# A four-layer graph network on one core: the vectors' pair products of the last two node parts move from VectorE to GpSimd, and their three-component sum is made by TensorE transposes

## The chip, the cores and the metric

The kernel is one program on one core of a Trainium2 chip. The metric is the device time of one execution in microseconds (us), lower is better. A core has five engines that run their own instruction streams and meet only at semaphores: TensorE (PE, matmuls and transposes into PSUM), VectorE (DVE), ScalarE (ACT), GpSimd (POOL) and SyncE (SP, which here only issues DMAs).

## What is computed

Four graph layers follow each other over 6,250 nodes and 206,250 edges. A node has 160 features: 64 scalars and 32 vectors of 3 components. Each layer ends in a residual and a layer norm. The last two layers (called L2 and L3 in the reference) have an edge part, which sums messages into each node, and a node part, which multiplies every node's own features with what it received. The node part of L3, cut to what matters:

```
a0 = agg[:, :64]                       # received scalars
a1 = agg[:, 64:].reshape(n, 32, 3)     # received vectors
xs = node_features[:, :64]
xv = node_features[:, 64:].reshape(n, 32, 3)
u0 = einsum('nu,nv,uvw->nw', xs, a0, Wu_ss) * INV64
   + einsum('nui,nvi,uvw->nw', xv, a1, Wu_vv) * (INV_SQRT3 * INV32)
u1 = einsum('nu,nvi,uvw->nwi', xs, a1, Wu_sv) * INV_SQRT2048
   + einsum('nui,nv,uvw->nwi', xv, a0, Wu_vs) * INV_SQRT2048
u0 = u0 + xs @ Lu_s * INV8
u1 = u1 + einsum('nui,uw->nwi', xv, Lu_v) * INV_SQRT32
x  = layernorm(x + node_features + update)
```

The term of this study is the second one of `u0`: for every node, the products of 32 own vectors with 32 received vectors, component by component, summed over the 3 components and then contracted with `Wu_vv`. L2 has the same term.

## The kernel before

The two node parts are two calls of `nodes_update`, named n3 and n4 (the trace writes both as `n_`). Each call goes over 50 blocks of 128 nodes, two blocks per turn of a hardware loop (`run_steps`). The engines' programs are software pipelined over blocks: in a step with number s, TensorE, VectorE, ScalarE and GpSimd do the front of block s, the products of block b = s - 1 and the end of block p = s - 2. Nothing but semaphores and the order in which each engine's program is written sets the order.

For one block b, with its 128 nodes on the 128 partitions:

- **Scalar pairs.** VectorE forms `n_ss`, the 64 x 64 products of own and received scalars, in four pieces of 1024 (`pair_products`, L1940). TensorE turns each piece by 128 x 128 transposes into `n_ps_s` (`turn_half`, L1803), ScalarE copies that to `n_turnedT` (L1899), and TensorE contracts it with the weights `n_WQ` into `n_ps_l` (`contract_half`, L1814). Two halves h come from each piece, so h runs from 0 to 7.
- **Vector pairs.** VectorE forms `n_vv`, 3 x 32 x 32 products, in one instruction of 3072 elements per partition (L1945). TensorE makes two more halves of it, h = 8 and 9: each 128 x 128 column block of each of the three components is multiplied with the identity, and the three products add up in PSUM (L1807). Copy and contraction follow as for the other halves.
- **End of block p** (`finish`, on VectorE). The sums of block p are added up into `n_y` (L1954, L1958), then comes the layer norm: statistics (L739, L741, L742), the inverse root on GpSimd (`inverse_root`, L757, a power of -0.5), and `n_new` (L747), which reads `n_y` and the statistics and waits for GpSimd's root.
- **Vector outputs** (`vector_products`, on VectorE). Two times: two products of a PSUM tile `n_ps_z` with a broadcast operand (L1974) and a reduction of 3072 elements to 48 (L1979). TensorE fills `n_ps_z` in `columns` (L1827).
- **Front of block s.** SP loads its rows into `n_row` (L1753), after L1954 of block p, which used that buffer. GpSimd copies the block's received sums into `n_own` (L1918), TensorE transposes both (`front`, L1774 to L1778), and `messages` (L1787, L1789) makes `n_agg`.

VectorE's program in a step is therefore `pair_products(b)`, `finish(p)`, `vector_products(b)`. GpSimd's is the copy of `n_own` for s and the root for p:

```
if s.exists():
    if s.reuses(2):
        pool.wait_ge(turned, s.count(-1))
    pool.tensor_copy(own[s.j][:, :], acc[:, bass.ds(s.t() * CAT, CAT)]).then_inc(held, 1)
p = s.back(2)
if p.exists():
    inverse_root(pool, stats[p.j][:, 8:9], power[:, 0:1], squares, roots, p, 1, 1)
```

In TensorE's program `turn_half(b, h + 1)` stands ahead of `contract_half(b, h)`; the front of s comes after h = 6, and `columns(b, 2)`, `columns(b, 3)` and `messages(s)` after h = 7.

Of the kernel before, what the change touches and what calls it, by code (L numbers as in the profile page):

```python
# [8 lines left out]
ALU = mybir.AluOpType  # L9
# [3 lines left out]
P = 128  # L13
# [8 lines left out]
CS, CV = 64, 32  # L22
D = CS + 3 * CV
# [66 lines left out]
def run_steps(eng, step, lag, unroll, number, held=(), peel=1):  # L90


    turns = number // unroll
    assert turns * unroll == number and lag <= unroll
    for i in range(peel):
        for j in range(unroll):
            step(Tile(i, j, unroll, number))
    with eng.Fori(peel, turns) as i:
        registers = {(a, c): eng.snap(eng.to_reg(i * a + c)) for a, c in held} or None
        for j in range(unroll):  # L100
            step(Tile(i, j, unroll, number, 0, registers))
    for j in range(lag):
        step(Tile(turns, j, unroll, number))
# [10 lines left out]
def bcast(ap, shape):  # L114
    return ap.to_broadcast(list(shape))
# [634 lines left out]
def layernorm(dve, chain, y, stats, out, squares, roots, item, nth, each):  # L750
    moments(dve, chain, y, stats, squares)
    return normalise(dve, y, stats, out, roots, item, nth, each)


def inverse_root(pool, at, power, squares, roots, item, nth, each):
    pool.wait_ge(squares, item.count(nth, each))
    pool.tensor_tensor(at, at, power, ALU.pow).then_inc(roots, 1)  # L757
# [945 lines left out]
def nodes_update(nc, g, A, name, mats, x, acc, x_out, scales, message_scales):  # L1703
# [11 lines left out]
    HALVES = 10  # L1715
    CHUNKS = 5
    REST = CAT - 4 * P
    with Phase(nc, name) as ph:
        two = range(2)

        def pair(name, shape):
            return [ph.sb(f"{name}{k}", shape) for k in two]
        WZ, WQ, WL, WM = ph.sb("WZ", [P, 2 * CH]), ph.sb("WQ", [P, 40, CS]), ph.sb("WL", [P, 2, D]), ph.sb("WM", [P, CHUNKS, D])
        row, agg, a0T, rowT, accT, lastT = pair("row", [P, 2 * P]), pair("agg", [P, D]), pair("a0T", [P, P]), pair("rowT", [P, 2 * P]), pair("accT", [P, 4 * P]), pair("lastT", [REST, P])
        own, ss = pair("own", [P, CAT]), pair("ss", [P, SQ])
        vv = ph.sb("vv", [P, 3 * CV * CV])
# [12 lines left out]
        row_in, stored = (ph.sems_of(n, 2) for n in ("row_in", "stored"))  # L1739

        with nc.Block() as block:
# [21 lines left out]
            def _(pe):  # L1763
# [28 lines left out]
                def turn_half(b, h):  # L1792
                    if h < 8:
                        pe.wait_ge(ss_set, b.count(h // 2 + 1, 4))
                    else:
                        pe.wait_ge(vv_set, b.count(1))
                    if h >= 2 or b.reuses(1):
                        pe.wait_ge(half_sb, b.count(h - 1, HALVES))
                    for c in range(4):
                        to = ps_s[h % 2][:, c * P:(c + 1) * P]  # L1800
                        if h < 8:
                            at = (4 * (h % 2) + c) * P
                            ins = pe.transpose(to, ss[h // 2 % 2][:, at:at + P], g.ident[:, :])  # L1803
                        else:
                            at = (4 * (h - 8) + c) * P
                            for k in range(3):
                                ins = pe.matmul(to, vv[:, k * CV * CV + at:k * CV * CV + at + P], g.ident[:, :], start=k == 0, stop=k == 2)  # L1807
                    ins.then_inc(half_ps, 1)

                def contract_half(b, h):  # L1810
# [99 lines left out]
            @block.gpsimd  # L1910
            def _(pool):
                pool.wait_ge(blank, 1)

                def step(s):
# [4 lines that stand above are left out]
                    p = s.back(2)  # L1919
                    if p.exists():  # L1920
                        inverse_root(pool, stats[p.j][:, 8:9], power[:, 0:1], squares, roots, p, 1, 1)
                run_steps(pool, step, 2, 2, NB)

            @block.vector
            def _(dve):
                dve.memset(power[:, :], -0.5)
                dve.tensor_tensor(twice[:, :], g.ident[:, 0:CS], g.ident[:, CS:P], ALU.add)
                for k in two:
                    ins = dve.memset(row[k][:, D:2 * P], 0.0)
                ins.then_inc(blank, 1)  # L1930
                links = Linked(dve, linked, 4)

                def pair_products(b):
                    k = b.j
                    dve.wait_ge(row_in[k], b.dma())
                    dve.wait_ge(agg_set, b.count(1))
                    for q in range(4):
                        if q >= 2 or b.reuses(1):
                            dve.wait_ge(half_ps, b.count(2 * q - 2 if q >= 2 else 2 * q + 6 - HALVES, HALVES))
                        dve.tensor_tensor(ss[q % 2][:, :].rearrange("p (u v) -> p u v", u=16),  # L1940
                                          bcast(row[k][:, 16 * q:16 * (q + 1)].unsqueeze(2), (P, 16, CS)),
                                          bcast(agg[k][:, 0:CS].unsqueeze(1), (P, 16, CS)), ALU.mult).then_inc(ss_set, 1)
                    if b.reuses(1):
                        dve.wait_ge(half_ps, b.count(0, HALVES))
                    dve.tensor_tensor(vv[:, :].rearrange("p (c u v) -> p c u v", c=3, u=CV),  # L1945
                                      bcast(row[k][:, CS:D].rearrange("p (c u) -> p c u", c=3).unsqueeze(3), (P, 3, CV, CV)),
                                      bcast(agg[k][:, CS:D].rearrange("p (c v) -> p c v", c=3).unsqueeze(2), (P, 3, CV, CV)),
                                      ALU.mult).then_inc(vv_set, 1)

                def finish(b):  # L1950
                    k = b.j
                    links.start(b)
                    dve.wait_ge(folded, b.count(1))
                    dve.scalar_tensor_tensor(out=y[k][:, :], in0=row[k][:, 0:D], scalar=2.0, in1=ps_l[k][:, 0:D],  # L1954
                                             op0=ALU.mult, op1=ALU.add).then_inc(upd_set, 1)
                    dve.wait_ge(upd_set, b.count(1))
                    dve.wait_ge(reduced, b.count(2, 2))
                    links.link(dve.tensor_tensor(y[k][:, CS:D], y[k][:, CS:D], sums[k][:, :], ALU.add))  # L1958
                    if b.reuses(2):
                        dve.wait_ge(stored[k], b.value(16, 16 * b.off))  # L1960
                    layernorm(dve, links, y[k][:, :], stats[k], new[k][:, :], squares, roots, b, 1, 1).then_inc(new_set, 1)
                    links.link(dve.memset(stats[k][:, 21:22], 0.0))
                    links.end()

                def vector_products(b):
                    k = b.j
                    out = prod[:, :].rearrange("p (c w t) -> p c w t", c=3, t=2 * CV)
                    for n in range(4):
                        dve.wait_ge(z_ps, b.count(n + 1, 4))
                        half, term = n // 2, n % 2  # L1970
                        if half or b.reuses(1):
                            dve.wait_ge(reduced, b.count(half - 1 + 1 if half else 0, 2))
                        other = (row if term else agg)[k][:, CS:D].rearrange("p (c m) -> p c m", c=3)
                        dve.tensor_tensor(out[:, :, :, term * CV:(term + 1) * CV],  # L1974
                                          bcast(ps_z[term][:, :].rearrange("p (w m) -> p w m", w=16).unsqueeze(1), (P, 3, 16, CV)),
                                          bcast(other.unsqueeze(2), (P, 3, 16, CV)), ALU.mult).then_inc(z_used, 1)
                        if term:
                            dve.wait_ge(z_used, b.count(n + 1, 4))
                            dve.tensor_reduce(sums[k][:, :].rearrange("p (c w) -> p c w", c=3)[:, :, 16 * half:16 * (half + 1)],  # L1979
                                              out, AX.X, ALU.add).then_inc(reduced, 1)  # L1980

                def step(s):
                    b, p = s.back(1), s.back(2)
                    if b.exists():
                        pair_products(b)
                    if p.exists():
                        finish(p)
                    if b.exists():
                        vector_products(b)
                run_steps(dve, step, 2, 2, NB)  # L1990
# [176 lines left out]
```

## Time and profile before

| | us |
|---|---|
| median of 3 runs | 21244.48 (21201.72 to 21290.81) |
| the profiled execution, its own time | 21241.17 |
| span of its trace | 21239.5 |
| PE busy | 17764.3 (84%) |
| DVE busy | 16408.4 (77%) |
| ACT busy | 11695.0 (55%) |
| POOL busy | 12354.7 (58%) |

Busy shares are averages over parts with very different limits. The two node parts of this study lie at about 16300 to 17620 us and 19910 to 21239.5 us of the span; the edge parts lie between and before them. A busy PE is not a PE at its peak, since its matmuls are pipelined and their ends are modelled. Spans on POOL are rough.

### The profile page before, as it was taken

The page shows a single profiled execution, that of the slowest core. Times are in us where ns is not written, and L with a number is a line of the kernel's source. Part 1 is how long each engine was busy: PE and PEld are TensorE (multiplying, and loading weights), DVE is VectorE, ACT ScalarE, POOL GpSimd, SP SyncE. Part 2 cuts the span into 40 slices and gives each one's busy share as a digit, 9 for nine tenths or more (in the row PEclk, how much of TensorE's full clock was granted, in tenths as well). Part 3 has the DMA queues.
Part 4 walks back from the last instruction along what each step waited for, and adds up shares of the span by engine and source line. Part 5 has one row for each costly group of instructions (what it writes and reads, how often), then busy time and mean ns, then how long its engine had stood idle before and what let it go on. Part 6 is the DMA issues. An engine that isn't in the chain of part 4 may idle for free. (4 is left out here: it accounts for less than half of the span.)

```text
span 21239.5 us, 463275 instructions
## 1 busy us (share of the span) xinstructions
PE 17764.3 (84%) x121874; PEld 14187.1 (67%) x121874; DVE 16408.4 (77%) x45070; ACT 11695.0 (55%) x37578; POOL 12354.7 (58%) x13048
## 2 busy tenths in 40 slices
PE   2777666656569999999999999879998888999888
PEld 1333322222258888888888888779997668999766
DVE  3777788888758888888899888765555886555688
ACT  1222244444437777777777777547775225777422
POOL 2777666656537767666677676447774005777300
PEclk8887788888889999999999999999999999999999
DMA  2666555555674444444444444432223002222200
GB/s 85 172 170 171 152 112 111 110 108 111 101 238 122 123 122 123 122 122 122 122 123 123 123 122 123 129 96 67 67 67 47 6 6 51 67 67 67 34 6 6
DMA packets 1922899, 2132.27 MB, mean 100 GB/s; under 512 B 745585, under 2 KB 1597713, under 8 KB 1922545
## 3 DMA queue, kind: packets, MB, share of 16 engines
q0 software_dynamic: 567456, 1314.26, 23.5%
q1 hardware_dynamic: 1355344, 816.91, 16.1%
q8 instruction: 36, 0.59, 0.0%
q14 instruction: 63, 0.51, 0.0%
HBM read 1518.49 MB, written 611.44 MB: 100 GB/s over the span
## 5 line engine op out<-in xcount | busy, mean ns | idle before, releaser
L1625 POOL DMA_INDIRECT e_rows<-x,e_take x3456 | 3338.6, 966 | 1155.0 <-issue 1071.4
L1659 ACT ACTIVATE e_hot<-e_hot,e_here 128x128 f32<-128x128 f32 x10368 | 3123.2, 387 | 1403.9 <-DVE e_hot L1682 1385.5
L629 PE MATMUL e_sums<-e_feat,e_same 128*128 128x480 f32 x3456 | 1958.0, 722 | 1335.7 <-DVE e_feat L697 1335.7
L1645 PE MATMUL e_sums<-e_rows,e_hot 128*128 128x128 f32 x20736 | 2882.1, 275 | 0.0
L613 POOL DMA_INDIRECT e_rows<-table,e_take x1728 | 1932.1, 1118 | 1321.2 <-issue 1287.5
L1645 PEld LDWEIGHTS e_sums<-e_rows,e_hot 128*128 128x128 f32 x20736 | 2682.3, 192 | 0.0
L629 PEld LDWEIGHTS e_sums<-e_feat,e_same 128*128 128x128 f32 x3456 | 799.5, 244 | 2494.1 <-issue 2402.2
L1200 ACT ACTIVATE e_m<-e_th,e_yt 128x64 f32<-128x64 f32 x6480 | 2300.8, 426 | 0.0
L648 ACT ACTIVATE e_feat<-e_feat,e_pay 128x64 f32<-128x64 f32 x5184 | 1284.7, 334 | 1768.6 <-DVE e_feat L672 1735.7
L1062 POOL DMA_INDIRECT e_srow<-src_table,e_at x1620 | 1612.4, 995 | 925.9 <-issue 917.7
L1073 POOL DMA_INDIRECT comb<-e_crow,e_at x1620 | 1669.2, 1030 | 803.2 <-issue 508.0
L757 POOL TENSOR_TENSOR n_stats<-n_stats,n_power 128x1 f32<-128x1 f32 x250 | 145.0, 580 | 3159.6 <-DVE n_stats L742 3072.4
L1065 POOL DMA_INDIRECT e_crow<-comb,e_at x1620 | 1666.5, 1029 | 493.8 <-issue 449.0
L327 POOL DMA_INDIRECT pay_rows<-order_stage,order_put x1620 | 1580.3, 976 | 496.4 <-issue 369.4
L1106 PE MATMUL e_ps_m<-ident,e_m 128*128 128x128 f32 x12960 | 1801.6, 283 | 26.8 <-DVE e_m L1338 8.5
L1641 PE MATMUL e_sums<-e_rows,e_hot 128*128 128x160 f32 x6912 | 1579.4, 310 | 205.3 <-ACT e_hot L1659 93.8
L1682 DVE TENSOR_TENSOR e_hot<-e_iota,e_here 128x512 f32<-128x512 f32 x864 | 599.4, 694 | 1301.9 <-PE e_sums L1645 1301.9
L1106 PEld LDWEIGHTS e_ps_m<-ident,e_m 128*128 128x128 f32 x12960 | 1497.8, 149 | 85.6 <-DVE e_m L1338 10.5
L1642 PE MATMUL e_sums<-e_rows,e_hot 128*128 128x160 f32 x6912 | 1508.2, 300 | 0.0
L1131 PE MATMUL e_ps_h<-e_WV,e_m2T 128*128 128x32 f32 x9720 | 1311.8, 272 | 0.0
L1693 DVE TENSOR_TENSOR acc<-acc,e_sums 128x320 f32 x1728 | 843.4, 488 | 523.0 <-issue 274.1
L421 ACT ACTIVATE order_stage<-order_ps_w 128x448 f32<-128x448 f32 x810 | 441.0, 544 | 1454.6 <-PE order_ps_w L389 1454.6
(330 smaller groups left out, 46394.2 us busy)
## 6 DMA issues: line engine op xcount, KB each, us to landing
e_pay<-pay_rows SPq DMA_DIRECT2D x432, 470.0 KB, 3.9
order_keys<-key_row SPq DMA_DIRECT2D x810, 128.0 KB
e_keys<-key_row SPq DMA_DIRECT2D x810, 128.0 KB, 3.4
comb<-n_comb SPq DMA_DIRECT2D x600, 164.0 KB, 2.0
e_rows<-x,e_take POOLq DMA_INDIRECT x3456
order_feat<-in_attr_T SPq DMA_DIRECT2D x810, 64.0 KB
e_basis<-in_attr_T SPq DMA_DIRECT2D x1620, 32.0 KB
e_comps<-in_attr_T SPq DMA_DIRECT2D x1620, 32.0 KB
```

The source lines that it names most:

```text
L327: pool.indirect_dma_start(out=pay_rows, out_offset=bass.IndirectOffsetOnAxis(ap=put[t.j // 2][:, 2 * (t.j % 2) + q:2 * (t.j % 2) + q + 1], ...
L613: pool.indirect_dma_start(out=rows[t.j][:, q, 0:D], out_offset=None, in_=table, in_offset=bass.IndirectOffsetOnAxis(ap=take[t.j][:, q:q + ...
L629: ins = pe.matmul(sums[b][q // G][:, 0:AGG0], same[b][:, q, :], feat[b][:, q, 0:AGG0], start=q % G == 0, stop=q % G == G - 1)
L1062: pool.indirect_dma_start(out=srow[n.j % 3][:, q, :], out_offset=None, in_=src_table, in_offset=bass.IndirectOffsetOnAxis(ap=at[n.j][:, q: ...
L1065: pool.indirect_dma_start(out=crow[n.j][:, q, 0:COMB], out_offset=None, in_=combs[2 * n.j + q][0:NP, :], in_offset=bass.IndirectOffsetOnAx ...
L1073: pool.indirect_dma_start(out=combs[2 * w.j + q], out_offset=bass.IndirectOffsetOnAxis(ap=at[w.j][:, 4 + q:5 + q], axis=0), in_=crow[w.j][ ...
L1106: ins = pe.transpose(ps_m[q][:, c * P:(c + 1) * P], m[n.j % 2][:, q, c * P:(c + 1) * P], g.ident[:, :])
L1200: ins = act.activation(m2[k][:, q, c * P:c * P + CS], th[k][:, q, 0:CS], ACT.Identity, scale=y, bias=y)
L1625: pool.indirect_dma_start(out=rows[t.j][:, q, 0:D], out_offset=None, in_=x, in_offset=bass.IndirectOffsetOnAxis(ap=take[t.j][:, q:q + 1], ...
L1641: pe.matmul(to[:, 0:D], one[:, q, 0, :], row[:, q, 0:D], start=first, stop=last)
L1645: ins = pe.matmul(bass.AP(o.tensor, o.offset, [o.ap[0], [DOT - CS * c, 2], [1, CS]]), one[:, q, 2 + c, :], bass.AP(r.tensor, r.offset, [r. ...
L1659: ins = act.activation(one[:, q, 2 + c, :], one[:, q, 0, :], ACT.Copy, scale=here[t.j][:, q, TOWARDS + c:TOWARDS + c + 1])
```

## The change

GpSimd forms `n_vv` instead of VectorE. It does so in its own step, after the root of block p. It waits there for the block's rows, for `n_agg`, and for TensorE to have turned the last of the previous block's halves, since `n_vv` is one buffer. In `turn_half` the multiplications with the identity become transposes (`is_transpose=True`), still with `start` at the first component and `stop` at the third.

```
                         else:
                             at = (4 * (h - 8) + c) * P
                             for k in range(3):
-                                ins = pe.matmul(to, vv[:, k * CV * CV + at:k * CV * CV + at + P], g.ident[:, :], start=k == 0, stop=k == 2)
+                                ins = pe.matmul(to, vv[:, k * CV * CV + at:k * CV * CV + at + P], g.ident[:, :], is_transpose=True,
+                                                start=k == 0, stop=k == 2)
                     ins.then_inc(half_ps, 1)
...
                     p = s.back(2)
                     if p.exists():
                         inverse_root(pool, stats[p.j][:, 8:9], power[:, 0:1], squares, roots, p, 1, 1)
+                    b = s.back(1)
+                    if b.exists():
+                        k = b.j
+                        pool.wait_ge(row_in[k], b.dma())
+                        pool.wait_ge(agg_set, b.count(1))
+                        if b.reuses(1):
+                            pool.wait_ge(half_ps, b.count(0, HALVES))
+                        pool.tensor_tensor(vv[:, :].rearrange("p (c u v) -> p c u v", c=3, u=CV),
+                                           bcast(row[k][:, CS:D].rearrange("p (c u) -> p c u", c=3).unsqueeze(3), (P, 3, CV, CV)),
+                                           bcast(agg[k][:, CS:D].rearrange("p (c v) -> p c v", c=3).unsqueeze(2), (P, 3, CV, CV)),
+                                           ALU.mult).then_inc(vv_set, 1)
...
-                    if b.reuses(1):
-                        dve.wait_ge(half_ps, b.count(0, HALVES))
-                    dve.tensor_tensor(vv[:, :].rearrange("p (c u v) -> p c u v", c=3, u=CV),
-                                      bcast(row[k][:, CS:D].rearrange("p (c u) -> p c u", c=3).unsqueeze(3), (P, 3, CV, CV)),
-                                      bcast(agg[k][:, CS:D].rearrange("p (c v) -> p c v", c=3).unsqueeze(2), (P, 3, CV, CV)),
-                                      ALU.mult).then_inc(vv_set, 1)
```

GpSimd's program in the loop of `nodes_update`, before the change (`n_own` is the copied block, `n_stats` with `n_power` the root; ISA and REGISTER_ALU rows are waits and the arithmetic for them):

```order
L98 ISA
L1918 ISA
L1918 COPY n_own<-acc 128x544
L757 TENSOR_TENSOR n_stats<-n_stats,n_power 128x1
L1918 ISA
L1918 COPY n_own<-acc 128x544
```

The same place after the change:

```order
L98 ISA
L1919 ISA
L1919 COPY n_own<-acc 128x544
L757 TENSOR_TENSOR n_stats<-n_stats,n_power 128x1
L1926 REGISTER_ALU
L1929 ISA
L1930 TENSOR_TENSOR n_vv<-n_row,n_agg 128x3072
L1919 ISA
L1919 COPY n_own<-acc 128x544
```

The new instruction stands between the root of block p and the next step's copy, which before followed the root directly.

VectorE's program in the same loop, from the last piece of scalar pairs into the layer norm, before the change:

```order
L1940 TENSOR_TENSOR n_ss<-n_row,n_agg 128x1024
L1945 TENSOR_TENSOR n_vv<-n_row,n_agg 128x3072
L1954 SCALAR_TENSOR_TENSOR n_y<-n_row,n_ps_l 128x160
L1958 TENSOR_TENSOR n_y<-n_y,n_sums 128x96
L739 BN_STATS n_stats<-n_y 128x6
```

The same place after the change:

```order
L1952 TENSOR_TENSOR n_ss<-n_row,n_agg 128x1024
L1960 SCALAR_TENSOR_TENSOR n_y<-n_row,n_ps_l 128x160
L1964 TENSOR_TENSOR n_y<-n_y,n_sums 128x96
L739 BN_STATS n_stats<-n_y 128x6
L740 MEMSET n_stats 128x1
```

The 3072-element product is gone from VectorE, and the end of block p follows the scalar pairs at once. TensorE's order is the same before and after.

## Rows read from the trace of the kernel before

**Rows 1.** The page's first line: the span.
```profile
span 21239.5 us, 463275 instructions
```

**Rows 2.** Windows: start:end, us, busy time (instructions) of each engine, clock, DMA.
```profile
16350.00:17580.00 1230.00, 1101.31 (x9459) 833.44 (x9457) 1098.55 (x900) 363.89 (x753) 53.49 (x95) 1.00 0.02 6
19960.00:21230.00 1270.00, 1137.29 (x9749) 860.88 (x9747) 1133.86 (x927) 373.69 (x773) 54.55 (x96) 1.00 0.02 6
```

**Rows 3.** Timeline of VectorE, one step: start us, us, what, [idle before <-releaser].
```profile
16810.85 3.70 DVE L1940 TENSOR_TENSOR n_ss<-n_row,n_agg 128x1024 f32<-128x1024 f32 x3
16816.07 1.23 DVE L1940 TENSOR_TENSOR n_ss<-n_row,n_agg 128x1024 f32<-128x1024 f32 x1 [1.52 <-PE n_ps_s L1803]
16817.21 3.35 DVE L1945 TENSOR_TENSOR n_vv<-n_row,n_agg 128x3072 f32<-128x3072 f32 x1
...
16822.71 0.65 DVE L747 TENSOR_SCALAR n_new<-n_y,n_stats 128x160 f32<-128x160 f32 x1 [0.66 <-POOL n_stats L757]
...
16823.57 1.76 DVE L1974 TENSOR_TENSOR n_prod<-n_ps_z,n_agg 128x1536 f32<-128x1536 f32 x1 [0.21 <-DVE n_stats L1962]
...
16830.41 1.76 DVE L1974 TENSOR_TENSOR n_prod<-n_ps_z,n_agg 128x1536 f32<-128x1536 f32 x1
...
16837.14 1.22 DVE L1940 TENSOR_TENSOR n_ss<-n_row,n_agg 128x1024 f32<-128x1024 f32 x1
```

**Rows 4.** Line 1945 in n3, then in n4: count, ns min/median/max, first and last start.
```profile
L1945 DVE TENSOR_TENSOR n_vv<-n_row,n_agg x50: 3349/3351/3355, 16323.6 to 17600.9; 128x3072 f32<-128x3072 f32 x50
L1945 DVE TENSOR_TENSOR n_vv<-n_row,n_agg x50: 3349/3351/3355, 19934.7 to 21213.3; 128x3072 f32<-128x3072 f32 x50
```

**Rows 5.** Timeline of GpSimd in the same step.
```profile
16822.12 0.55 POOL L757 TENSOR_TENSOR n_stats<-n_stats,n_power 128x1 f32<-128x1 f32 x1 [25.15 <-DVE n_stats L742]
16822.62 0.64 POOL L1918 COPY n_own<-acc 128x544 f32 x1
```

**Rows 6.** Line 747: in n4, in the first node part, and in n3's end (timeline).
```profile
L747 DVE TENSOR_SCALAR n_new<-n_y,n_stats x50: 362/650/666, 19963.5 to 21234.7; 128x160 f32<-128x160 f32 x50
L747 DVE TENSOR_SCALAR n_new<-n_y,n_stats x50: 361/362/365, 5851.7 to 6237.6; 128x160 f32<-128x160 f32 x50
17606.24 0.36 DVE L747 TENSOR_SCALAR n_new<-n_y,n_stats 128x160 f32<-128x160 f32 x1 [0.66 <-POOL n_stats L757]
```

**Rows 7.** Timeline of the first node part, VectorE beside GpSimd.
```profile
5893.12 0.58 DVE L961 TENSOR_SCALAR n_nrm<-n_new,n_stats 128x64 f32<-128x64 f32 x1 [0.90 <-POOL n_stats L757]
5893.55 0.59 POOL L912 COPY n_agg<-acc 128x480 f32 x1
5902.88 1.01 DVE L963 TENSOR_TENSOR n_nrm<-n_nrm,n_gam 128x160 f32<-128x160 f32 x1
5903.10 0.59 POOL L912 COPY n_agg<-acc 128x480 f32 x1
```

**Rows 8.** Groups of GpSimd by line and form, whole span: count, busy us, mean ns.
```profile
L1918 POOL COPY n_own<-acc 128x544 f32 x96 | 61.1, 637 | 44.4 <-PE n_ps_a L1778 44.4
L912 POOL COPY n_agg<-acc 128x480 f32 x46 | 27.3, 594 | 0.1
```

**Rows 9.** Timeline of TensorE in the step of rows 3.
```profile
16812.20 1.09 PE L1803 MATMUL n_ps_s<-ident,n_ss 128*128 128x128 f32 x8 [0.81 <-DVE n_ss L1940]
...
16822.95 0.44 PE L1774 MATMUL n_ps_t<-ident,n_row 128*128 128x128 f32 x2 [1.64 <-DMA n_row<-x]
...
16823.77 2.84 PE L1807 MATMUL n_ps_s<-ident,n_vv 128*128 128x128 f32 x24
...
16827.13 0.69 PE L1827 MATMUL n_ps_z<-n_WZ,n_rowT 64*128 64x512 f32 x1
```

**Rows 10.** Timeline of TensorE and a window, second node part.
```profile
13722.48 3.61 PE L1463 MATMUL n_ps_m<-n_runs,ident 128*128 128x164 f32 x24 [1.63 <-DVE n_runs L1526]
13736.98 5.28 PE L1463 MATMUL n_ps_m<-n_runs,ident 128*128 128x164 f32 x24 [2.29 <-DVE n_runs L1526]
13735.00:13752.00 17.00, 12.44 (x60) 11.48 (x60) 9.59 (x33) 1.03 (x4) 1.10 (x2) 0.80 0.73 172
```

## The prediction

> **What bounds the kernel now.** I read the busy time in windows first. In the two steady stretches of the node parts [rows 2] VectorE is busy for 1098.55 of 1230 us and 1133.86 of 1270 us, 89% of both, TensorE for 90% at a granted clock of 1.00, GpSimd for 4%. So VectorE or the loop that it closes with TensorE should set the step. The timeline of VectorE [rows 3] settles it. A step goes from the first piece of scalar pairs at 16810.85 to that of the next block at 16837.14, 26.29 us. The one wait on TensorE is the 1.52 us ahead of the last scalar piece. The layer norm's stall is 0.66 us for GpSimd's root. Everything else is back to back, and ahead of the next step's first row no idle time is listed. VectorE is the bound, and each us that its chain gains or loses counts, once per block. Line 1945 has 50 rows per part [rows 4]; first to last start divided by 49 is 26.07 us per step in n3 and 26.09 us in n4. That makes 98 steady steps, and 1 us per step is 98 us.
>
> **What goes and what moves, on VectorE.** I write t0 for a step's start (16810.85 in [rows 3]). The product leaves VectorE. It took 3.35 us by its own row; the end of block p stood 3.27 us behind its start, since neighbours overlap by 0.08. So the end of block p starts 3.27 us earlier, and so does GpSimd's root: from 16822.12 [rows 5], t0 + 11.27, to t0 + 8.00. Taken alone that would be 98 x 3.27 = 320 us off the time. The scalar pairs before it still wait for TensorE as they do now.
>
> **What is added, on GpSimd: the place.** The moved product stands directly behind the root, where the next step's copy stood. In [rows 5] that copy begins at 16822.62, not later than the recorded end of the root (16822.12 + 0.55 = 16822.67), although a semaphore wait stands between them. All the new product's waits are satisfied long before: the block's rows and `n_agg` were needed by the scalar pairs, and the last half of the block before was turned in the step before. So it should begin where the copy began, t0 + 8.50 after the shift.
>
> **What it does to VectorE there.** VectorE's next instruction is `n_new` (L747, which normalises the result of L1958), which waits for the same root. Before, its record starts at 16822.71, 0.09 us after the copy's, and lasts 0.65 us. The median in n4 is 650 ns, while in the first node part, where no copy follows the root, it is 362 ns, and at the end of n3, with no block left to copy, it is 0.36 us [rows 6]. It ends at 16823.36, and the copy at 16823.26: it ends 0.10 us behind the copy. The first node part shows the same with other operations: a product of two SBUF tensors takes 1.01 us and ends at 5903.89, 0.20 us behind a copy that ends at 5903.69 [rows 7]. So I read that `n_new` cannot move its data while GpSimd works on SBUF. Behind the new product it then waits for the whole product, not for 0.64 us.
>
> The Trainium skill, SBUF — State Buffer, "Who interferes with whom", says that VectorE and GpSimd share one pair of ports under an exclusive lock which is held for the whole instruction, and that one-tensor operations in a two-port mode and products with two SBUF inputs fall under it. By that rule the trace's 650 against 362 ns is the lock, and the rule speaks against this change.
>
> **Its length, T.** No row has a two-input product of this size on GpSimd. The nearest are copies [rows 8]: 637 ns for 544 elements, 594 ns for 480. Scaled by length, a copy of 3072 would take 3.6 us; that is the low end, one operand read. With two operands read one after the other it is twice that, 7.2 us, the high end. The product has two operands, so I stay near the upper end, a little below because scaling counts the copy's fixed part more than five times: T = 6.8 us, an estimate.
>
> The Trainium skill, GPSIMD Engine Reference, section 3.1, gives 4497 ns for a two-input add of 2048 elements. An estimate from it is 6.75 us for 3072, and with that the sum below would be 5 us smaller.
>
> **The sum.** The product ends at t0 + 8.50 + T. `n_new` ends 0.10 us later, and the first vector product starts 0.21 us after that [rows 3]: t0 + 8.81 + T. From there to the next step it is 16837.14 - 16823.57 = 13.57 us, VectorE's own work back to back. The step becomes 22.38 + T, against 26.29 now, a change of T - 3.91 us. With T = 6.8 it is +2.89 us, 98 times 283 us. In the first step of each part there is no end of a block; there the product starts beside the scalar pairs, which have two SBUF inputs too, so VectorE loses T and gains 3.27: 3.5 us each, 7 us together. Sum +290 us on 21241.17 us, the execution that the rows come from (its span is 21239.5 us [rows 1], 1.67 us lie around it), is 21531; the median of the runs lies 3 us above that execution. I say 21530 us.
>
> **What costs nothing, and why.** *TensorE's halves 8 and 9:* 12 multiplications are 24 records in 2.84 us, while 8 transposes of scalar pairs are 8 records in 1.09 us [rows 9]. Twelve transposes should take about 1.6 us; 1.2 us off for each of two halves, 2.4 us per step. This lies in a wait. TensorE is ready for the front of block s at 16822.95 - 1.64 = 16821.31, t0 + 10.46, where it now waits for the row's DMA, issued behind the end of block p. That DMA comes 3.27 us earlier, so the wait goes, and TensorE reaches half 8 at about t0 + 11.3. The product is there at t0 + 15.3: the stall becomes 4.0 us, and the transposes start beside `n_new`. *`columns`:* now they start 3.36 us after half 8 does, then 2.1 us after it, t0 + 17.4, before VectorE has used both PSUM tiles; they are needed at t0 + 22.5. No loss. *Queued behind the product on GpSimd:* the copy for block s + 1 (TensorE wants it over 20 us later) and the next root, at t0 + 8 of the next step. The product has ended over 20 us before that too. No loss, except for the port, below.
>
> **Rivals.**
> 1. *The copy goes first.* At the product's end the waiting `n_new` and GpSimd's next copy both want to go on. Against it: an operation at 5893.12 took 0.58 us, ending at 5893.70, inside the copy that had begun at 5893.55. For it: the product at 5902.88 started before the copy of 5903.10 and still ended behind it [rows 7]. Price 0.64 us a step, 63 us: 21595 us. Chance 0.28.
> 2. *`n_new` slips in ahead of the product (the other side).* Then VectorE is not held: its vector products start near t0 + 9.2 and are half done near t0 + 16. The product starts at about t0 + 8.95, ends at 15.75, `columns` start 2.1 us later and need some 1.2 us, and VectorE's second half, which takes 6.73 us [rows 3], waits until t0 + 19.1. Step 25.8 us, -0.5 us: about 21190 us, not slower. It decides if GpSimd needs more than 0.1 us longer to start behind the root than it needs for the copy; the new product has more waits ahead of it. Against it: GpSimd has the 0.55 us of the root to work them off, and the copy won at the median of n4 [rows 6]. Chance 0.10.
> 3. *T is near the copy's rate.* With 3.6 us the step changes by -0.31 us, 21210 us; no change on balance up to T = 3.9. Chance of anything below 4.9 us (+0.5%): 0.06.
> 4. *TensorE's clock falls.* It now stands at 1.00 with waits of 1.64 us; it will wait for 4.0 us. In a stretch granted 0.80, 24 records took 5.28 us instead of 3.61 [rows 10], 46% more. TensorE's 23.3 us per step, less 2.4, would be 30.5 us at that rate, more than the new step; with some 3 us a step more it is about 21820 us. Against it: in the node parts the clock stays at 1.00 (2.4 GHz) over the waits that there are, and most of what TensorE does has slack then. Chance 0.06.
>
> **How the numbers follow.** Forecast as summed: 0.50. This measurement tells 0.5%, 106 us, from no change. Forecast and rivals 1 and 4 are slower: 0.84. Rival 3 and most of rival 2 are within 0.5%: 0.11. Rival 2 is faster by over 0.5% only with T below 6.2 us: 0.05. The range holds the forecast and rival 1. From above: T = 7.2 with the copy first gives +3.93 us, 21634 us, and 45 us for a product dearer than two copies. From below: T = 5.4 gives +1.5 us, 21390 us. What lies outside is rivals 2 to 4.
>
> **What would show it.** Right: about 100 rows of GpSimd with `n_vv`, 128x3072, near 6.8 us, starting within 0.1 us of the root's end; `n_new` with a median near 6.8 us instead of 650 ns, ending 0.1 us behind them (0.74 if the copy goes first); VectorE's busy time up although it does less; steps of 29.2 us; halves 8 and 9 as 12 records; ScalarE and TensorE waiting some 4 us ahead of half 8; the edge parts unchanged. Wrong: `n_new` at 362 ns with waits of VectorE for `n_ps_z` (rival 2), a product under 5 us, or a clock below 0.95 in the windows of the node parts.

## The result and the profile after

| | median us | runs |
|---|---|---|
| before | 21250.26 | 21201.72 to 21290.81, 4 runs |
| changed | 21523.25 | 21432.36 to 21538.45, 4 runs |

The ratio is 1.012, 95% interval 1.0099 to 1.0142: the change made the kernel 1.2% slower, between 210 and 302 us. The forecast was 21530 us. Here and below, ratios and intervals compare fast executions only; one of the kernel before, at 23226 us, ran in a slower state of the chip and is left out.

The windows of the two steady stretches of the changed kernel answer to [rows 2]:

```profile
16507.00:17701.00 1194.00, 977.89 (x7381) 695.50 (x7380) 1033.13 (x753) 324.77 (x668) 271.90 (x126) 0.91 0.02 6
20230.00:21432.00 1202.00, 980.39 (x7384) 696.82 (x7383) 1034.10 (x753) 325.27 (x669) 271.92 (x126) 0.91 0.02 6
```

GpSimd's busy share went from 4% to 23%, as it should. TensorE's busy share went from 90% to 82%, and its granted clock from 1.00 to 0.91, a mixture of its two levels. The clock is not part of the forecast's sum.

The line of `n_new` in such a stretch gives the length of a step: the last start less the first, divided by the count less one. Here before, and then changed (count, ns min/median/max, first and last start):

```profile
L747 DVE TENSOR_SCALAR n_new<-n_y,n_stats x41: 649/650/653, 16457.0 to 17502.4; 128x160 f32<-128x160 f32 x41
```

```profile
L747 DVE TENSOR_SCALAR n_new<-n_y,n_stats x42: 5390/5393/5396, 16519.3 to 17693.2; 128x160 f32<-128x160 f32 x42
L1930 POOL TENSOR_TENSOR n_vv<-n_row,n_agg x50: 5355/5363/6401, 16373.4 to 17780.0; 128x3072 f32<-128x3072 f32 x50
```

The step was (17502.4 - 16457.0) / 40 = 26.14 us and is (17693.2 - 16519.3) / 41 = 28.63 us in n3; in n4 it is 28.84 us by the same reckoning. That is 2.60 us more on average, times 98 is 254 us, inside the 210 to 302 us of the ratio. The steps are the better measure of the change. The traces differ ahead of n3 as well, where no kernel of this study changes anything: the first `n_new` of n3 starts at 16352.4 us before and at 16407.3 us in the changed kernel, and at 16288 to 16416 us over all of them.

The timeline of VectorE in one step of the changed kernel answers to [rows 3]:

```profile
16871.15 3.62 DVE L1952 TENSOR_TENSOR n_ss<-n_row,n_agg 128x1024 f32<-128x1024 f32 x3
16877.73 1.23 DVE L1952 TENSOR_TENSOR n_ss<-n_row,n_agg 128x1024 f32<-128x1024 f32 x1 [2.96 <-PE n_ps_s L1803]
...
16880.92 5.39 DVE L747 TENSOR_SCALAR n_new<-n_y,n_stats 128x160 f32<-128x160 f32 x1 [0.67 <-POOL n_stats L757]
...
16886.52 1.76 DVE L1980 TENSOR_TENSOR n_prod<-n_ps_z,n_agg 128x1536 f32<-128x1536 f32 x1 [0.21 <-DVE n_stats L1968]
...
16900.09 2.35 DVE L1952 TENSOR_TENSOR n_ss<-n_row,n_agg 128x1024 f32<-128x1024 f32 x2
```

GpSimd in the same step, which answers to [rows 5]:

```profile
16880.33 0.55 POOL L757 TENSOR_TENSOR n_stats<-n_stats,n_power 128x1 f32<-128x1 f32 x1 [22.47 <-DVE n_stats L742]
16880.85 5.36 POOL L1930 TENSOR_TENSOR n_vv<-n_row,n_agg 128x3072 f32<-128x3072 f32 x1
16886.15 0.65 POOL L1919 COPY n_own<-acc 128x544 f32 x1
```

And TensorE, which answers to [rows 9]:

```profile
16874.56 1.11 PE L1803 MATMUL n_ps_s<-ident,n_ss 128*128 128x128 f32 x4
...
16878.21 0.66 PE L1803 MATMUL n_ps_s<-ident,n_ss 128*128 128x128 f32 x4
...
16886.26 1.53 PE L1807 MATMUL n_ps_s<-ident,n_vv 128*128 128x128 f32 x12 [2.37 <-POOL n_vv L1930]
```

VectorE's waits for scalar halves in n3 and n4 of the changed kernel (us in total, times, longest), against 61.2 and 61.5 us for 41 steps before:

```profile
DVE n_ss L1952 <- PE n_ps_s L1803: 108.0, 56, 3.0
DVE n_ss L1952 <- PE n_ps_s L1803: 115.4, 59, 3.0
```

What the reader is to see: the product starts at 16880.85, when the root ends (16880.88). `n_new` starts 0.07 us behind it and ends at 16886.31, 0.10 us after the product's 16886.21. From the first vector product (16886.52) to the next step there are 13.57 us, as before. But the wait for TensorE ahead of the last scalar piece is 2.96 us instead of 1.52, and TensorE's own rows show why: four transposes of scalar pairs took 1.11 us at 16874.56 and 0.66 us at 16878.21. The same kind of instruction ran at two clocks within one step.

### The profile page after: what moved, and what is told of

It reads as the page before. It is cut to its first block and busy times, and to the rows that moved or that the text cites. A ratio compares the mean times of both kernels' runs of the same rounds, so it can differ in the third digit from the quotient of the medians.

```text
span 21536.8 us, 458671 instructions
## 1 busy us (share of the span) xinstructions
PE 17758.7 (82%) x119474; PEld 14086.1 (65%) x119474; DVE 16550.3 (77%) x44970; ACT 11694.6 (54%) x37578; POOL 12883.2 (60%) x13148
## 5 line engine op out<-in xcount | busy, mean ns | idle before, releaser
L1900 ACT ACTIVATE n_turnedT<-n_ps_s 128x512 f32<-128x512 f32 x1000 | 590.7, 597 | 1396.0 <-PE n_ps_s L1803 939.4
```

## The experiments

"The port" below is short for what holds `n_new` back while GpSimd works on SBUF, as the prediction reads it. "Half" and "piece" are those of the scalar and vector pairs above.

All times below are compared with the kernel before on the same chip; the chips differ among themselves (its median was 21249 us beside the first four kernels, 21250 beside the next four, 21179 beside the last two), so the ratios count. Steps are of n3, worked out from `n_new`'s line as above.

| kernel | median us | ratio (95%) | step us | clock | `n_new` us | wait for `n_ps_s` per step us |
|---|---|---|---|---|---|---|
| before | | 1 | 26.14 | 1.00 | 0.65 | 1.49 |
| changed | 21523 | 1.012 (1.0099 to 1.0142) | 28.63 | 0.91 | 5.39 | 2.57 |
| both_products | 22036 | 1.0377 (1.0345 to 1.0408) | 34.14 | 0.85 | 5.39 | 4.73 |
| product_after_new | 21279 | 1.001 (0.9991 to 1.0029) | 26.51 | 0.90 | 0.36 | 1.52 |
| pool_matmul | 21357 | 1.0076 (1.0048 to 1.0103) | 27.68 | 0.95 | 5.39 | 1.56 |
| vector_transpose | 21371 | 1.0064 (1.0038 to 1.0089) | 27.57 | 0.93 | 0.65 | 3.06 |
| transpose_twice | 21203 | 0.9983 (0.9967 to 0.9998) | 26.12 | 1.00 | 0.65 | 1.48 |
| three_pieces_matmul | 21421 | 1.0074 (1.0051 to 1.0097) | 28.19 | 0.92 | 1.94 | 2.38 |
| early_transpose | 21143 | 0.9945 (0.9921 to 0.9969) | 24.72 | 0.93 | 0.36 | 2.83 |
| early_matmul | 21096 | 0.9919 (0.9894 to 0.9945) | 24.84 | 1.00 | 0.36 | 1.48 |
| changed_filler | 21331 | 1.0075 (1.0049 to 1.0101) | 27.57 | 1.00 | 5.40 | 1.48 |
| early_filler | 20941 | 0.9889 (0.9871 to 0.9908) | 23.44 | 1.00 | 0.36 | 1.48 |

The last column is the sum of VectorE's waits for `n_ps_s` in the stretch over the number of `n_new` in it.

**both_products.** Is it the port that costs, or the late product? Here nobody waits for GpSimd's product.

```
                         inverse_root(pool, stats[p.j][:, 8:9], power[:, 0:1], squares, roots, p, 1, 1)
+                    b = s.back(1)
+                    if b.exists():
...
+                        pool.tensor_tensor(idle[:, :].rearrange("p (c u v) -> p c u v", c=3, u=CV),
...
+                                           ALU.mult).then_inc(idle_set, 1)
```

(The refill of `n_row` and of `n_agg` also waits for it. In the trace neither is held by it: what SyncE waits for last ahead of the refill is `n_y`, and what ScalarE waits for last ahead of `n_agg` is TensorE.)

> The kernel before, in which GpSimd behind the root also forms the same product into a buffer that nobody reads (TensorE still takes VectorE's product by multiplications with the identity). Theory (the port: n_new is held as long as GpSimd works on SBUF, 5.36 us): n_new about 5.4 us instead of 0.65, the step 26.1 + 4.7 = 30.8 us, 98 steps +465 us, about 21710 us, a little more if TensorE's clock falls too. Rival (the change lost its time because TensorE waits for a late product, not by the port): nobody waits for the product here, so n_new stays at 0.65 us and the time at about 21250 us.

Its `n_new`, its window, and VectorE's wait for TensorE (us in total, times, longest):

```profile
L747 DVE TENSOR_SCALAR n_new<-n_y,n_stats x43: 5390/5395/5401, 16477.5 to 17911.3; 128x160 f32<-128x160 f32 x43
16476.00:17935.00 1459.00, 1234.13 (x8558) 903.82 (x8555) 1201.41 (x813) 328.21 (x681) 278.45 (x129) 0.85 0.02 5
DVE n_ss L1956 <- PE n_ps_s L1806: 203.2, 84, 3.5
```

`n_new` is held for the whole of a product whose result it doesn't need and nobody reads: that GpSimd's work as such holds VectorE is shown. But the step grew by 8.0 us, not by 4.7. The rest stands in the third row: 203.2 / 43 = 4.73 us per step of waiting for scalar halves, 3.24 us more than before, at a clock of 0.85. TensorE's program is that of before; all that changed for it is that it stands idle longer. 4.75 + 3.24 = 7.99 us.

**product_after_new.** The other way round: the product is needed, but does not meet `n_new`.

```
                         pool.wait_ge(row_in[k], b.dma())
+                        if p.exists():
+                            pool.wait_ge(new_set, p.count(1))
                         pool.wait_ge(agg_set, b.count(1))
```

> The changed kernel, but GpSimd starts the product only when n_new of block p is done. Theory (the port): n_new falls to 0.36 us; the product runs from about t0 + 9.0 to t0 + 14.4, columns start 2.1 us later and take 1.2 us, VectorE's second half of 6.73 us starts at t0 + 17.7: step 24.4 us at full clock, about 21090 us; with 1 us for the clock 21190 us. Rival (GpSimd's product is simply too long wherever it stands): the step stays at 28.8 us and the time at 21520 us, since the product now even starts 0.5 us later.

`n_new` fell to 0.36 us, and the time to that of before although the product starts later: the price on VectorE was the port's. The step is not the 24.4 us that were worked out at full clock, nor the 25.4 with an allowance. VectorE now waits 4.0 us per step for `n_ps_z`, and TensorE, granted 0.90, runs late from half 8 to `columns`. In the step shown, the twelve transposes of half 8 took 2.82 us, against 1.53 us in the step of the changed kernel above. That is 1.3 of the 2.1 us; no run tells the rest apart:

```profile
L747 DVE TENSOR_SCALAR n_new<-n_y,n_stats x41: 361/362/365, 16409.1 to 17469.3; 128x160 f32<-128x160 f32 x41
16406.00:17495.00 1089.00, 938.68 (x7278) 663.12 (x7275) 812.70 (x742) 317.83 (x658) 266.24 (x123) 0.90 0.02 6
DVE n_prod L1982 <- PE n_ps_z L1828: 163.5, 41, 4.6
16812.67 2.82 PE L1807 MATMUL n_ps_s<-ident,n_vv 128*128 128x128 f32 x12 [2.94 <-POOL n_vv L1932]
```

**pool_matmul and vector_transpose.** Each half of the change alone: the product on GpSimd with the multiplications kept, and the transposes with the product on VectorE. The edits are the diff's two parts.

> The changed kernel with the multiplications with the identity instead of the transposes. Theory 1 (the transposes only shorten work that lies in a wait): 2.6 us more TensorE work per step, hidden behind n_new's and VectorE's time: 21520 us, same as the changed kernel. Theory 2 (the step's extra 1 us over 22.38 + 5.36 us is TensorE's clock, and it falls because TensorE does less per step): the granted clock in the node parts rises from 0.91 and the time falls by 30 to 100 us, to 21420 to 21490 us.

> The kernel before with the transposes alone, the product still on VectorE. Theory 1: TensorE's 2.6 us per step were hidden: 21250 us, same as before, clock 1.00 in the node parts. Theory 2 (less TensorE work lets the clock fall): the granted clock in the node parts falls below 0.97 and VectorE's waits for n_ps_s grow, 20 to 100 us more than before.

```profile
L1929 POOL TENSOR_TENSOR n_vv<-n_row,n_agg x50: 5355/5363/6397, 16256.8 to 17623.3; 128x3072 f32<-128x3072 f32 x50
16394.00:17545.00 1151.00, 1028.32 (x8378) 789.55 (x8376) 1030.95 (x751) 323.43 (x669) 270.18 (x125) 0.95 0.02 6
```

```profile
16503.00:17641.00 1138.00, 960.51 (x7330) 675.69 (x7329) 962.20 (x782) 324.35 (x663) 46.70 (x82) 0.93 0.02 6
DVE n_ss L1941 <- PE n_ps_s L1803: 125.5, 75, 3.3
```

Theory 2 holds in both, and more strongly than expected. The transposes alone, which take work away and touch nothing on VectorE, make the kernel 0.64% slower. What they save on TensorE gathers in its wait for the first scalar pairs, which is 2.5 us at its longest there and 1.1 us before. The move without them costs 1.54 us per step, near the T - 3.91 = 1.45 us that the forecast's formula gives for T = 5.36 us; with them it costs 2.49.

**transpose_twice.** Is it the kind of the instruction, or TensorE's idle time? Each group of three transposes is done twice over the same columns, so that their time is that of the multiplications.

```
-                            for k in range(3):
+                            for k in [0, 1, 2, 0, 1, 2]:
```

> The kernel before (product on VectorE) with transposes, each group of three done twice over the same PSUM columns, so that halves 8 and 9 have 24 records each again, as with the multiplications. Theory 1 (the clock fell in vector_transpose because TensorE had 2.6 us less to do per step): TensorE's busy time is back at 90% of the step, the clock at 1.00, the step at 26.1 us, the time at 21250 us. Theory 2 (transposes hold the clock less than multiplications do, whatever time they take): the clock stays at 0.93 or lower with TensorE as busy as before, the step at 27.5 us or more, the time at 21370 us or more.

```profile
L747 DVE TENSOR_SCALAR n_new<-n_y,n_stats x41: 648/650/653, 16427.8 to 17472.7; 128x160 f32<-128x160 f32 x41
16423.00:17493.00 1070.00, 951.77 (x8232) 714.96 (x8231) 955.86 (x779) 316.54 (x655) 46.66 (x82) 1.00 0.02 6
```

Theory 1. With work that is thrown away in the place of the work saved, the clock is at 1.00 and the step at 26.12 us. So it was the time that TensorE no longer filled that let the clock fall, not the transposes as such.

**changed_filler.** If that is so, the changed kernel must lose its extra 1.1 us when its waits are filled. (The wait for the PSUM tile stands ahead of the filler.)

```
+                    if h in (0, 8):
+                        for c in range(16):
+                            pe.transpose(ps_s[h % 2][:, c % 4 * P:(c % 4 + 1) * P], g.ident[:, :], g.ident[:, :])
                     if h < 8:
                         pe.wait_ge(ss_set, b.count(h // 2 + 1, 4))
```

> The changed kernel, with 16 transposes of the identity matrix, whose result is overwritten, in each of TensorE's two long waits (ahead of half 0, some 2.5 us, and ahead of half 8, some 2.4 us). Theory (the 1 us per step of the changed kernel over 22.38 + 5.36 us is TensorE's clock, and it falls because TensorE stands idle): clock 0.95 or higher, VectorE's waits for n_ps_s back to 1.5 us, step 27.7 to 27.9 us, 21370 to 21400 us. Rival (the extra waits are the transposes' own, or work on TensorE only costs): the step stays at 28.7 us or grows by the filler, 21520 us or more.

```profile
L747 DVE TENSOR_SCALAR n_new<-n_y,n_stats x42: 5395/5401/5405, 16398.5 to 17528.8; 128x160 f32<-128x160 f32 x42
16388.00:17532.00 1144.00, 1052.79 (x8692) 771.09 (x8691) 1029.00 (x750) 321.74 (x665) 269.46 (x125) 1.00 0.02 6
DVE n_ss L1955 <- PE n_ps_s L1806: 62.2, 42, 1.5
```

The clock is 1.00, the wait is 1.48 us, and the step is 27.57 us. The formula with the measured T gives 26.14 + 1.45 = 27.59 us. What is left against before is the port's price, to within 0.02 us.

**three_pieces_matmul.** Is VectorE let go at the end of one instruction of GpSimd, or only when no further one is queued? pool_matmul with the product in three instructions, one component each.

```
+                        for c in range(3):
+                            part = slice(CS + c * CV, CS + (c + 1) * CV)
+                            pool.tensor_tensor(vv[:, c * CV * CV:(c + 1) * CV * CV].rearrange("p (u v) -> p u v", u=CV),
...
```

> pool_matmul with GpSimd's product in three instructions of one component, 1024 elements, each. Theory (VectorE gets the port at the end of the instruction that holds it, ahead of GpSimd's next one, as n_new did ahead of the copy in the changed kernel): n_new about 1.9 us instead of 5.39; TensorE waits for the third piece, and VectorE's second half for columns: step 25.5 us, about 21190 us. Rival (GpSimd keeps the port through instructions that are queued): n_new stays at 5.4 us or more and the time at 21360 us or more.

```profile
L747 DVE TENSOR_SCALAR n_new<-n_y,n_stats x42: 1937/1941/1945, 16487.4 to 17643.1; 128x160 f32<-128x160 f32 x42
```

```profile
L1931 POOL TENSOR_TENSOR n_vv<-n_row,n_agg x150: 1901/1912/2943, 16340.5 to 17730.2; 128x1024 f32<-128x1024 f32 x150
16475.00:17648.00 1173.00, 1048.75 (x8382) 813.09 (x8380) 889.58 (x753) 323.63 (x669) 282.12 (x209) 0.92 0.02 6
DVE n_prod L1980 <- PE n_ps_z L1827: 133.7, 41, 4.3
16718.71 5.49 PE L1807 MATMUL n_ps_s<-ident,n_vv 128*128 128x128 f32 x24 [2.85 <-POOL n_vv L1931]
```

`n_new` is released at the end of the first piece, 1.91 us, though GpSimd has the next one queued. The pieces follow each other without a gap (three of them took 5.65 us in one step), so the rows don't tell how the two share the moment between. The expected time was wrong, though. The step is 28.19 us, slower than pool_matmul's. VectorE is free earlier and then waits 3.2 us per step for `n_ps_z`, since TensorE still waits for the whole product, and what follows runs at the lower clock: the 24 records of half 8 took 5.49 us in the step shown, against 2.84 us in [rows 9]. The window's row is a warning, too. TensorE is busy for 89% of it, as before the change, at a clock of 0.92: records that run slowly fill the time, and the busy share alone doesn't show the loss.

**early_transpose and early_matmul.** The product stands ahead of the root, in two alternating buffers; `n_own`'s copy waits for `n_new`.

```
+                        if s.reuses(3):
+                            pool.wait_ge(new_set, s.count(-2))
                         pool.tensor_copy(own[s.j][:, :], acc[:, bass.ds(s.t() * CAT, CAT)]).then_inc(held, 1)
+                    b = s.back(1)
+                    if b.exists():
...
+                        if b.reuses(2):
+                            pool.wait_ge(half_ps, b.count(-HALVES, HALVES))
+                        pool.tensor_tensor(vvs[k][:, :].rearrange("p (c u v) -> p c u v", c=3, u=CV),
...
                     p = s.back(2)
                     if p.exists():
                         inverse_root(pool, stats[p.j][:, 8:9], power[:, 0:1], squares, roots, p, 1, 1)
...
-                run_steps(pool, step, 2, 2, NB)
+                run_steps(pool, step, 2, 2, NB, peel=2)
```

(With `peel=2` GpSimd's loop starts one turn later, and the steps ahead of it are written out.)

> The product of block b stands ahead of the root of block p on GpSimd, in two alternating buffers, so that it starts as soon as n_agg is there (t0 - 5.0) and ends near t0 + 0.4, under VectorE's second reduction; the copy of n_own waits for n_new. Transposes as in the changed kernel. Theory (the port held at n_new is the change's price on VectorE, and TensorE's clock the rest): n_new 0.36 us, VectorE's chain 22.9 us per step; at full clock 20950 us, with a clock near 0.9 and 1.5 to 2.5 us more waiting for TensorE 21090 to 21190 us. Rival (a product of 5.4 us on GpSimd costs wherever it stands, since the scalar pairs read two SBUF tensors): the step stays above 26 us, 21250 us or more.

> early_transpose with the multiplications with the identity. TensorE has 23.4 us of work per step, so it becomes the bound or nearly: step 24.5 to 25.3 us at a clock of 1.00, 21090 to 21170 us. Theory 2 of the clock (multiplications hold it up): not slower than early_transpose although TensorE does 2.6 us more. If only TensorE's time counts, early_transpose is the faster one by 100 us or more.

Both are faster than before, by 0.55% and 0.81%. Their steps are almost the same, 24.72 and 24.84 us, for opposite reasons: with the transposes the clock is 0.93 and VectorE waits 2.83 us per step for halves; with the multiplications the clock is 1.00, but `n_agg` comes later against VectorE's step, so that the product reaches further into the scalar pairs. There the port costs as well: the first three pieces take 6.06 us of a timeline in early_matmul, 4.69 us in early_transpose, against 3.70 us before.

```profile
16797.89 5.36 POOL L1929 TENSOR_TENSOR n_vv<-n_row,n_agg 128x3072 f32<-128x3072 f32 x1 [8.73 <-ACT n_a0T L1888]
16802.13 4.69 DVE L1954 TENSOR_TENSOR n_ss<-n_row,n_agg 128x1024 f32<-128x1024 f32 x3
```

```profile
16813.18 5.36 POOL L1928 TENSOR_TENSOR n_vv<-n_row,n_agg 128x3072 f32<-128x3072 f32 x1 [10.10 <-ACT n_a0T L1887]
16816.05 6.06 DVE L1953 TENSOR_TENSOR n_ss<-n_row,n_agg 128x1024 f32<-128x1024 f32 x3
```

What VectorE does beside the rest of the product is not held. In early_transpose a product from PSUM and a reduction beside GpSimd's next product take 1.75 and 3.35 us, what they take without it:

```profile
16820.81 1.75 DVE L1982 TENSOR_TENSOR n_prod<-n_ps_z,n_row 128x1536 f32<-128x1536 f32 x1
16821.42 5.36 POOL L1929 TENSOR_TENSOR n_vv<-n_row,n_agg 128x3072 f32<-128x3072 f32 x1 [8.48 <-ACT n_a0T L1888]
16822.59 3.35 DVE L1987 TENSOR_REDUCE n_sums<-n_prod 128x48 f32<-128x3072 f32 x1
```

**early_filler.** Both findings together: early_transpose, with the filler of changed_filler ahead of half 0 only.

> early_transpose with the same 16 filler transposes ahead of half 0 only, where TensorE waits 2.7 us for the first scalar pairs. Theory: the clock rises from 0.93 to 1.00, VectorE's waits for n_ps_s fall from 2.8 to 1.5 us, step 24.7 - 1.3 = 23.4 us, 20990 to 21040 us, faster than every kernel so far. Rival: the filler runs into the wait's end and delays half 0: step 24.7 us or more, 21140 us.

```profile
L747 DVE TENSOR_SCALAR n_new<-n_y,n_stats x40: 360/363/364, 16429.7 to 17343.9; 128x160 f32<-128x160 f32 x40
16413.00:17353.00 940.00, 893.14 (x7740) 663.59 (x7739) 830.18 (x723) 309.59 (x641) 262.32 (x120) 1.00 0.02 7
```

The step is 23.44 us, 2.70 us less than before, and the kernel is 1.1% faster than before (0.9889, 0.9871 to 0.9908). It is the fastest of all that were run. It uses the change's own two ideas; what differs is where GpSimd's product stands, and that TensorE is kept from idling.

## Why the prediction was right, and where it was not

- **VectorE bounds the step, and 13.57 us follow `n_new`:** right, to the hundredth in [rows 3] and in the timeline after.
- **Where the product starts:** right. Forecast: with the copy's start, not later than the root's recorded end; measured 16880.85 against 16880.88. Counted from the step's start it is 9.70 us and not 8.50, mainly because of the longer wait ahead of the last scalar piece (2.96 instead of 1.52 us).
- **`n_new` is held until 0.10 us after the product:** right, 16886.31 against 16886.21, and both_products and product_after_new show that it is the port. The Trainium skill, SBUF — State Buffer, "Who interferes with whom", says the same; the traces agree with 5.39 us beside a product of 5.36, and 0.36 us without one.
- **T = 6.8 us:** the term was mis-sized. It is 5.36 us, between the bounds of 3.6 and 7.2. The reading that a second operand nearly doubles the copy's price was too dear. That is 1.44 us per step, 141 us too much. (It is still above the 4.9 us below which rival 3 lay.) The estimate of 6.75 us from the Trainium skill, GPSIMD Engine Reference, section 3.1, is too high by nearly as much; here both operands are read with repeats, one of them each element 32 times in a row, and no run tells whether that is why.
- **"What costs nothing": the transposes.** This step failed. The saved time lies in a wait, as the prediction said, and for that very reason it was not free: the clock fell to 0.91, the first halves came later, and VectorE waited 1.08 us (n3) and 1.25 us (n4) more per step, 114 us over 98 steps. pool_matmul, vector_transpose, transpose_twice and changed_filler show it from four sides. The prediction had weighed TensorE's work by time alone, and looked for a cost only where a product or `columns` would come late.
- **Rival 4, the clock:** it came true in kind, at a chance of 0.06 and with a third of the price per step. The clock of 0.91 is below the 0.95 that the prediction itself named as a sign of being wrong. The rival had been tied to the wait for the product; the transposes were the larger part, since without them the clock is 0.95 and its price 0.1 us (27.68 against 27.59 us).
- **Rival 1:** it did not happen. The copy's row is 0.65 us, and `n_new` ended while it ran, 0.10 us behind the product and not 0.74.
- **Rival 2:** not by itself. Built on purpose (product_after_new) it gave 0.1% more than before, within the measurement's uncertainty.

So the total came out within 7 us of the median by luck: two errors of opposite sign nearly cancel, 141 us too much for the product, some 114 us too little for the clock. The direction did not hang on either: the move itself, with the clock at 1.00, makes the kernel 0.75% slower (changed_filler).

## What to carry to other kernels

Work that is moved from VectorE to GpSimd isn't gone from VectorE as long as VectorE has something to do meanwhile that GpSimd's work holds, as `n_new` and the scalar pairs were held here: ask what VectorE does at that moment, and put the product under something that isn't held, here the products from PSUM and the reductions. Work that is taken off TensorE can cost time even where TensorE waits. In these runs a TensorE that was left with longer waits was granted less, and the stretch that others do wait for ran slower. By how much the clock falls for how much idle time is not worked out here; read the granted clock in the windows before and after, and try the same change with the wait filled. A forecast that meets the measured total should still be checked term by term.

## What was not expected of the hardware

- Twelve records fewer in each of two halves, 2.6 us less work per step in all, took the granted clock of a stretch from 1.00 to 0.93 and cost 1.43 us per step on another engine (vector_transpose); 16 transposes of the identity, 1.9 us of discarded work in a wait, brought it back from 0.93 to 1.00 and the step from 24.72 to 23.44 us (early_filler).
- With TensorE's program unchanged and only its wait longer, the clock was 0.85 and the price 3.24 us per step (both_products), more than half of what the wait itself cost.
- GpSimd's product took 5.36 us for 3072 elements and 1.91 us for 1024: 1.69 ns per element and some 0.2 us besides. Its first one of each part took 6.40 us.
- `n_new` is held only until GpSimd's running instruction ends, not until those queued behind it have (three_pieces_matmul, 1.94 us beside three pieces of 1.91 us).
